# Token routing and dispatch in two sets, with the start of layer 2 for one set laid beside the last expert units, and expert weights loaded by DMA

## The chip, the core and the metric

The kernel runs on one core of a Trainium2 chip. A core has TensorE (PE, matmuls and transposes), VectorE (DVE), ScalarE (ACT, functions by table), GpSimd (POOL), and SyncE (SP), which issues most of the DMAs here. Each engine works through its own queue of instructions in program order, and engines wait for each other at semaphores. The metric is the time of one execution on the device, in microseconds (us); lower is better.

## The reference

The input is x, 16 sequences of 256 tokens of 128 floats (4096 tokens, all fp32). Two layers follow, both of the form x = x + s * silu(g) on normalised xn.

```python
xn = _layernorm(x)
# layer 0: attention per sequence; f is query, key and value
f = xn @ W.T + b
s = softmax(f @ f.T + distance_bias) @ f
# layer 0: a shared FFN and 8 routed experts, top 2 of sigmoid(logits)
shared = (silu(xn @ shared_gate.T) * (xn @ shared_up.T)) @ shared_down.T
w = top-2 scores per token, normalised to sum 1
combined = sum over the token's two experts: w * ((silu(xn @ gate_w) * (xn @ up_w)) @ down_w)
x = x + s * silu(shared + combined)
# layer 1 (called layer 2 below): token statistics attention, 16 heads of 8
xn = _layernorm(x)
w = xn @ Wqkv.T
logits = sum over d of (w / norm of w over the sequence)**2 * temp
Pi = softmax over heads(logits);  dots = sum over tokens of Pi_norm * w*w
s = (-(w * Pi) / (1 + dots)) @ Wout.T + bout
# layer 1: one expert per sequence, chosen by its last token
sel = argmax(softmax(gelu(last @ Wp1 + bp1) @ Wp2 + bp2))
out = (gelu(xn @ W1[sel] + b1) @ W2[sel] + b2) @ Wo + bo
x = x + s * silu(xn + 0.3 * out)
```

## The kernel before

**Tiles.** 4096 tokens are 32 tiles t of 128 (a token per partition), grouped in 8 chunks c of four tiles, which are two sequences b each. X holds x, XA the normalised tokens, XB a copy of them. Rows of XA and XB have 130 columns: 128 values, where the expert's result is to go, and the token's weight for it. XT is the transposed XA, FT and F are the projection f both ways, S the attention's output, SH the shared FFN's. PS0 to PS7 are the eight banks of PSUM.

**Order.** The order is written out by hand, engine by engine. Helpers of the same name on different engines are the parts of one step: `up(j)` is on TensorE the two matmuls of half a chunk, on ScalarE the SiLU (into SG), on VectorE the product (into HH).

1. *Start.* Per chunk: statistics (DVE L646), a root on ScalarE, `normalize` (DVE L657), four transposes (`turn_in`, PE L288, copied out by ScalarE), router logits (`logits`, PE L296), projection and its transpose (`project`, `turn_f`, PE L304 and L312). `spread_in`, `EARLY = 3` and `MID = 6` set which of them go before what.
2. *Routing.* When all 32 tiles have logits, VectorE finds the two experts of each token (`top`, twice, on 128x256 elements: 8 experts by 32 tiles), TensorE counts ranks with two matmuls (L329, L331), and VectorE turns them into places POS in a scratch buffer in DRAM (to L743), each expert's tokens padded to units of 128. EUI lists each unit's expert as an address (L749).
3. *Dispatch.* GpSimd scatters XA and XB, a tile at a time, in 64 indirect DMAs (L1230) into xs_scratch.
4. *Attention of layer 0*, 16 steps: scores on TensorE (L345), maximum on VectorE (L758 to L763), exponential on ScalarE (L1044), transposes (L357), `mix` (L370).
5. *Shared FFN*, the first `LATE = 5` chunks (PE L396 onwards).
6. *Experts.* SyncE fetches four units at a time (`fetch`) when all 64 scatters have landed. 71 units: transpose (`turn_x`, L441), eight gate and up matmuls per unit (L458; the "128x128 x568" in the profile), SiLU (ACT L1091), product (DVE L812), down matmuls (L472), output scaled (ACT L1098), scattered by GpSimd into yc_scratch (L1236). VectorE's `choose(u)` copies the unit's gate and up weights from WE, which holds all experts, into one of four buffers WC:

```python
r = e.value_load(EUI[0:1, u:u + 1], min_val=0, max_val=7 * 768)
e.tensor_copy(WC[:, u % 4, :], WE[:, bass.ds(r, 512)]).then_inc(s_wc, 1)
```

7. *Behind the experts.* The last three chunks of the shared FFN; 16 collects of yc; `end0(c)` adds the pairs of results and the shared part (DVE L823, L827) and takes the SiLU; GpSimd multiplies by S and, for odd chunks, adds into X (L1245).
8. *Head of layer 2*, all eight chunks in a pipeline: `stats1`, `norm1`, `turn1` (ACT L1131), `proj`, `squares` (two squares with a sum, ACT L1140, and a copy), `weigh`, `heads`, `center`, then the choice of 16 experts (`a1`, `a2`, SELI) and the softmax over heads (`soft`, `share`).
9. *Loop of layer 2*, b = 0 to 18, a sequence per step: `spread` every second step (PE transposes, ACT copy L1174, VectorE's sums L887 to L906), `out1` (PE L585), `ff_up` (L597), `ff_down` (L609), `ff_out`, `end_gate`, and the stores. SyncE loads each sequence's expert weights (`expert1`, 258 KB, L252).

## Time and profile before

| what | value |
|---|---|
| median of 3 runs | 371.18 us (369.55 to 375.51) |
| the profiled execution | 370.86 us, its span 369.0 us |
| TensorE busy | 301.6 us (82%) |
| VectorE busy | 222.2 us (60%) |
| ScalarE busy | 183.0 us (50%) |
| GpSimd busy | 184.1 us (50%) |
| granted TensorE clock, mean | 0.932 |

The span is the stretch from the first to the last instruction of the profiled execution, and its own time is 1.9 us above it. Busy shares are means over stages with different limits, so they say little alone: the rows below are by stage. The granted clock is the share of full speed (2.4 GHz) that TensorE was given; 0.5 is its lower level of 1.2 GHz.

### The profile page before, as it was taken

What the parts mean: (1) busy time and instruction counts of PE and PEld (TensorE: products, weight loads), DVE (VectorE), ACT (ScalarE), POOL (GpSimd) and SP (SyncE); (2) the same over time, 40 slices, a digit from 0 to 9 for tenths busy, and PEclk for the clock granted to TensorE, in tenths of its full rate; (3) what the DMA queues carried; (4) which work ended last, traced back from release to release, by engine and by line L of the source; (5) the groups of instructions that cost most, each with busy time, mean ns of one, the idle gap of its engine ahead of it and who ended that gap; (6) DMA issues with size and microseconds to landing.
All of it is one profiled execution on the core that took longest, in us unless ns stands there. A gap on an engine that the chain in (4) does not pass through costs nothing.

```text
span 369.0 us, 6792 instructions
## 1 busy us (share of the span) xinstructions
PE 301.6 (82%) x1933; PEld 250.9 (68%) x1933; DVE 222.2 (60%) x722; ACT 183.0 (50%) x482; POOL 184.1 (50%) x186
## 2 busy tenths in 40 slices
PE   0896599998998089999999999997448859987880
PEld 0684386776565079999999999865125647876770
DVE  5946846655222035555655555447999775778765
ACT  2356545555532025665565565523428765565450
POOL 1220277777777506666666577716965200142432
PEclk9999969999999759999999999998959967999996
DMA  6999931111111231332323232157000032234411
GB/s 195 248 208 146 370 143 54 54 56 51 51 52 51 68 91 35 108 106 70 105 73 105 67 103 65 37 186 272 1 0 0 1 95 55 81 110 103 136 57 57
DMA packets 33187, 35.66 MB, mean 97 GB/s; under 512 B 3824, under 2 KB 26482, under 8 KB 33024
## 3 DMA queue, kind: packets, MB, share of 16 engines
q1 hardware_dynamic: 28832, 26.76, 28.1%
q0 software_dynamic: 4320, 8.47, 6.9%
q8 instruction: 17, 0.28, 0.3%
q14 instruction: 18, 0.15, 0.1%
HBM read 19.87 MB, written 15.80 MB: 97 GB/s over the span
## 4 chain that ended last, share of the span: by engine, by line
PE 44%; DVE 22%; POOL 15%; issue 9%; ACT 4%; DMA 3%; SPq 1%; POOLq 0%; DVEq 0%
PE PS L458 18%; POOL xs_scratch L1230 15%; PE PS L472 9%; DVE XA L657 3%; PE PS L585 3%; DVE ST L646 2%; PE PS L441 2%; PE PS L609 2%; PE PS L296 2%; DVE XG L887 2%; DVE WE L906 2%; DVE SH L827 1%; PE PS L304 1%; PE PS L288 1%; DVE F L823 1%
## 5 line engine op out<-in xcount | busy, mean ns | idle before, releaser
L1236 POOL DMA_INDIRECT yc_scratch<-YS,XS x71 | 69.8, 983 | 45.5 <-ACT YS L1098 24.7
L458 PE MATMUL PS<-XG,XB 128*128 128x128 f32 x568 | 77.3, 281 | 0.7 <-ACT XG L1086 0.7
L458 PEld LDWEIGHTS PS<-XG,XB 128*128 128x128 f32 x568 | 71.4, 198 | 1.1 <-ACT XG L1086 1.1
L800 DVE COPY XB<-WE 128x512 f32 x71 | 30.9, 435 | 34.0 <-issue 33.1
L1091 ACT ACTIVATE FT<-PS 128x256 f32<-128x256 f32 x71 | 27.3, 384 | 39.8 <-PE PS L458 39.8
L812 DVE TENSOR_TENSOR FT<-FT,PS 128x256 f32<-128x256 f32 x71 | 29.9, 421 | 24.5 <-PE PS L472 16.4
L1230 POOL DMA_INDIRECT xs_scratch<-XA,POS x32 | 31.5, 983 | 26.4 <-DVE POS L743 17.0
L472 PE MATMUL PS<-WE,FT 128*128 x284 | 43.2, 275 | 0.2 <-DVE FT L812 0.2
L472 PEld LDWEIGHTS PS<-WE,FT 128*128 128x128 f32 x284 | 37.4, 192 | 0.4 <-issue 0.4
L1230 POOL DMA_INDIRECT xs_scratch<-XB,POS x32 | 31.3, 978 | 9.8 <-issue 9.8
L1258 POOL TENSOR_TENSOR F<-F,S 128x512 f32<-128x512 f32 x7 | 8.9, 1274 | 52.6 <-DVE F L937 52.6
L787 DVE TENSOR_TENSOR FT<-FT,PS 128x512 f32<-128x512 f32 x16 | 11.0, 687 | 29.2 <-PE PS L408 22.5
L1098 ACT ACTIVATE YS<-PS,XS 128x128 f32<-128x128 f32 x71 | 26.0, 366 | 3.9 <-PE PS L472 0.5
L1044 ACT ACTIVATE PR<-E,NM 128x256 f32<-128x256 f32 x32 | 16.0, 500 | 22.0 <-DVE NM L763 22.0
L370 PE MATMUL PS<-F,PT 128*128 128x128 f32 x128 | 18.9, 294 | 1.9
L441 PE MATMUL PS<-C,XS 128*128 128x128 f32 x71 | 11.6, 289 | 10.2 <-DMA XS<-xs_scratch 10.2
L370 PEld LDWEIGHTS PS<-F,PT 128*128 128x128 f32 x128 | 16.3, 200 | 5.0 <-DVE PT L772 5.0
L657 DVE TENSOR_SCALAR XA<-X,MV,RS 128x128 f32<-128x128 f32 x64 | 18.8, 357 | 0.6
L597 PE MATMUL PS<-XT,XS 128*128 128x256 f32 x64 | 18.2, 414 | 0.7 <-DMA XS<-in_w 0.7
L1245 POOL TENSOR_TENSOR F<-F,S 128x512 f32<-128x512 f32 x8 | 11.9, 1499 | 11.5 <-ACT F L1112 11.5
L345 PE MATMUL PS<-FT 128*128 128x256 f32 x64 | 17.6, 402 | 0.0
L609 PE MATMUL PS<-E,XS 128*128 128x256 f32 x64 | 17.0, 389 | 0.2 <-ACT PT L1192 0.2
(166 smaller groups left out, 600.4 us busy)
## 6 DMA issues: line engine op xcount, KB each, us to landing
xs_scratch<-ZB SPq DMA_DIRECT2D x1, 4680.0 KB, 28.6
XS<-xs_scratch SPq DMA_DIRECT2D x17, 260.0 KB
XS<-in_w SPq DMA_DIRECT2D x16, 258.0 KB, 2.9
WE<-in_we SPq DMA_DIRECT2D x1, 3072.0 KB, 16.7
X<-in_x SPq DMA_DIRECT2D x16, 128.0 KB, 2.4
XB<-yc_scratch SPq DMA_DIRECT2D x8, 256.0 KB, 4.4
WE<-yc_scratch SPq DMA_DIRECT2D x8, 256.0 KB, 6.0
out<-X SPq DMA_DIRECT2D x16, 128.0 KB, 2.1
```

Of the source, the lines that this page charges most:

```text
L370: m = e.matmul(PS[k][:, i * 128:(i + 1) * 128], PT[:, kb, j, i * 128:(i + 1) * 128], F[:, 2 * b + j, :], start=j == 0, stop=j == 1)
L441: m = e.transpose(PS[6][:, j * 128:(j + 1) * 128], XS[:, g % 4, j, 0:128], ident)
L458: m = e.matmul(PS[k][:, f * 128:(f + 1) * 128], WC[:, u % 4, f * 128:(f + 1) * 128], XG[:, g % 2, j * 128:(j + 1) * 128], start=True, stop ...
L472: m = e.matmul(PS[k][:, 0:128], HH[:, u % 3, f * 128:(f + 1) * 128], WE[:, bass.ds(reg[u] + (512 + f * 128), 128)], start=f == 0, stop=f == 1)
L609: m = e.matmul(PS[4][:, 0:256], WS[:, s, 256 + f * 128:256 + (f + 1) * 128], H1[:, b % 2, f, :], start=f == 0, stop=f == 1)
L657: m = e.tensor_scalar(XA[:, t, 0:128], X[:, t, :], MV[:, t, 0:1], RS[:, t:t + 1], ALU.subtract, ALU.mult)
L800: e.tensor_copy(WC[:, u % 4, :], WE[:, bass.ds(r, 512)]).then_inc(s_wc, 1)
L812: e.tensor_tensor(HH[:, u % 3, 0:256], SG[:, u % 3, 0:256], PS[u % 3][:, 256:512], ALU.mult).then_inc(s_hhe, 1)
L1091: e.activation(SG[:, u % 3, 0:256], PS[u % 3][:, 0:256], ACT.Silu, bias=0.0, scale=1.0).then_inc(s_sge, 1)
L1098: e.activation(YS[:, u % 8, :], PS[(5, 7)[u % 2]][:, 0:128], ACT.Copy, bias=0.0, scale=XS[:, g % 4, j, 129:130]).then_inc(s_ys, 1)
L1230: e.indirect_dma_start(out=xs, out_offset=bass.IndirectOffsetOnAxis(ap=POS[:, s, t:t + 1], axis=0), in_=T[:, t, :], in_offset=None, bounds ...
L1236: e.indirect_dma_start(out=yc, out_offset=bass.IndirectOffsetOnAxis(ap=XS[:, g % 4, j, 128:129].bitcast(U32), axis=0), in_=YS[:, u % 8, :] ...
```

## The change

**Two sets.** `CA = 4`: set 0 is the tokens of chunks 0 to 3, set 1 those of chunks 4 to 7. `choose(g)` (the top 2), `ranks(g)`, `positions(g)`, `experts(g)` and GpSimd's `dispatch(g)` exist for each set. Units of set 0 that are full come first (up to 32, `place(u)` gives a unit's place in the scratch), then eight units, one per expert, where set 0's remainders and set 1's first tokens share a unit, then set 1's. `FULL = 25`, `SHARED = 63`, `LAST_A = 40` (units whose results finish set 0) and `Y0 = 49` follow.

**Start and shared FFN.** TensorE, VectorE and ScalarE have a new order from the first chunk on. All eight chunks of the shared FFN come ahead of the attention, their `up` steps between the parts of the start. `project` and `turn_f` of chunks 4 to 7 stand in the attention's first steps. ScalarE makes the copies XB of chunks 4 to 7 (`copy_b`).

**Expert weights.** WE and VectorE's copies go. Down weights of all experts stay in WY; the gate and up weights of a unit are loaded by SyncE from DRAM (`weights(u)`, 256 KB) into the four buffers WC, at an address it reads from EI, once the unit four back is through. SyncE begins them after the last product and the last down of the shared FFN (`s_hh` 16, `p_dn` 8).

**Beside the last experts.** After unit 48's weights SyncE collects chunks 0 to 3. From unit 49 on VectorE does one part of `early(k)` behind each `hidden(u)` (the unit's product): per chunk `add_y`, `add_shared`, `gate_s`, `stats1`, and `norm1` of the chunk two back. ScalarE has the SiLU and two roots there.

**Behind the experts.** `norm1` of chunks 2 and 3 and layer 2's head for chunks 0 to 3 alone, then the loop. Adds, statistics, norms and head of chunks 4 to 7 stand behind the loop's steps b = 0 to 7, on VectorE, ScalarE and TensorE. GpSimd's products with S go to VectorE (`gate_s`). Eight head steps are done in one instruction per set. The buffers E, PR, PT lie in one tensor EP; ScalarE has 19 table loads in place of 8.

The first place is VectorE at the end of the routing: the places POS are ready, then the list of units' experts (in XG for a moment), and then comes the next step of the attention (L758).

```order
L739 TENSOR_REDUCE RW<-XS 128x32
L741 TENSOR_REDUCE RW<-XS 128x32
L743 CAST POS<-RW 128x64
L744 TENSOR_TENSOR XG<-C,RW 128x504
L747 TENSOR_REDUCE EU<-XG 128x72
L749 TENSOR_SCALAR EUI<-EU 128x72
L758 ISA E,RW<-PS,C 128x256
L758 ISA RW 128x1
```

In the changed kernel the same place is that of set 0. L753 is a product of the shared FFN, L734 and L737 are the norm of chunk 4.

```order
L878 TENSOR_REDUCE RW<-XS 128x16
L880 CAST POS<-RW 128x2x16
L753 TENSOR_TENSOR YS<-WC,PS 128x512
L888 TENSOR_TENSOR XG<-C,RB 128x504
L891 TENSOR_REDUCE EU<-XG 128x72
L899 TENSOR_SCALAR EI<-EU 128x72
L734 RECIPROCAL RS<-RS 128x4
L737 TENSOR_SCALAR XA<-X,MV,RS 128x128 x4
```

The shared FFN's product and the norms of chunks 4 to 7 now stand around and behind set 0's places, where the attention stood.

The second place is TensorE around the two rank matmuls (L329 and L331 before, L379 and L380 after). Before, projections (L304) and their transposes (L312) stand around them:

```order
L304 MATMUL PS4<-XT,WA 128x512
L312 MATMUL PS5<-C,FT 128x128 x4
L329 MATMUL PS7<-BFC 128x256
L331 MATMUL PS7<-BFC 128x256
L304 MATMUL PS3<-XT,WA 128x512
L312 MATMUL PS6<-C,FT 128x128 x4
```

After, L412 and L414 are the gate and up matmuls of the shared FFN, L355 the transposes of chunk 4's XA, L369 its logits:

```order
L390 MATMUL PS1<-XT,WA 128x512
L400 MATMUL PS7<-C,FT 128x128 x8
L379 MATMUL PS2<-BFC 128x128
L380 MATMUL PS2<-BFC 128x128
L412 MATMUL PS3<-XT,WB 128x512
L414 MATMUL PS4<-XT,WB 128x512
L355 MATMUL PS0<-C,XA 128x128 x4
L369 MATMUL PS7<-WA,XT 128x8 x4
L412 MATMUL PS5<-XT,WB 128x512
L414 MATMUL PS6<-XT,WB 128x512
```

Chunk 4's transposes, which were ahead of the ranks, now stand behind them and behind one `up` step, and each later chunk's logits follow its own transposes directly.

The third place is VectorE in the loop of layer 2. Before, the row L887 of a `spread` follows the FFN's part (L937, L914, L931) and the shares of a later chunk (L870 to L876) at once:

```order
L899 RECIPROCAL SM<-SM 128x2
L906 SCALAR_TENSOR_TENSOR WE<-PR,SM,FT 128x256 x2
L870 TENSOR_REDUCE WE<-WE 128x4
L872 RECIPROCAL WE<-WE 128x4
L876 TENSOR_TENSOR YS<-WE 128x512
L937 SCALAR_TENSOR_TENSOR F<-F,SH 128x512
L914 SCALAR_TENSOR_TENSOR S<-PS,WD 128x512
L931 SCALAR_TENSOR_TENSOR SH<-PS,SH 128x512
L887 ISA XG,SM<-PR,WE 128x256
```

After, at the end of step b = 2 and in b = 3 (L1111 and L1128 are the old L914 and L931):

```order
L975 TENSOR_TENSOR SH<-SH,F 128x512
L1111 SCALAR_TENSOR_TENSOR S<-PS1,WD 128x512
L1128 SCALAR_TENSOR_TENSOR SH<-PS7,SH 128x512
L981 TENSOR_TENSOR F<-F,S 128x512
L983 TENSOR_TENSOR X<-X,F 128x512
L726 BN_STATS ST<-X 128x6 x4
L729 BN_AGGR MV<-ST 128x2 x4
```

The adds of chunk 7 (L975) stand ahead of step 3's own work, and behind it `gate_s` and `stats1` of chunk 4; the last four rows come once more, for chunk 5, before the next `spread`.

The diff, cut to its core:

```diff
+CA = 4
+NTS = (4 * CA, NT - 4 * CA)
+FULL = 8 * CA - 7
+SHARED = NU - NE
+def place(u):
+    if u < 8 * CA:
+        return u
+    return u - 8 * CA + SHARED if u < 8 * CA + NE else u - NE
...
@@ SyncE
+            def weights(u):
+                if u >= 4:
+                    e.wait_ge(p_ge, u - 3)
...
+                    v = e.value_load(EI[0:1, g, place(u):place(u) + 1], min_val=0, max_val=7 * 256)
+                    of = D["wg"][bass.ds(v, 256)]
+                e.dma_start(WC[:, u % 4, :], of.rearrange("(p j) k -> p (j k)", j=2)).then_inc(d_wc[u % 4], 16)
...
-            e.wait_ge(d_disp, 16 * 2 * NT)
-            for g in range(NG):
-                fetch(g)
+            e.wait_ge(d_disp[0], 16 * 2 * NTS[0])
+            e.wait_ge(s_places, 2)
+            fetch(0)
+            e.wait_ge(s_experts, 1)
+            e.wait_ge(s_hh, 16)
+            e.wait_ge(p_dn, 8)
+            for u in range(4):
+                weights(u)
+            for g in range(1, 4):
+                fetch(g)
+            for u in range(4, NU):
+                weights(u)
+                g = u // 4 + 1
+                if u % 4 == 0 and 4 <= g < NG:
+                    fetch(g)
+                if u == LAST_A + 8:
+                    for i in range(8):
+                        e.wait_ge(d_y[i], 16 * (CA + 1))
+                    for c in chunks[0]:
+                        collect(c)
...
@@ TensorE
+            logits(3)
+            up(0)
+            up(1)
+            project(3)
+            turn_f(2)
+            turn_f(3)
+            ranks(0)
+            up(2)
+            turn_in(4)
+            logits(4)
+            up(3)
+            down(0)
+            turn_in(5)
+            logits(5)
+            up(4)
...
+            up(6)
+            up(7)
+            down(2)
+            ranks(1)
+            for j in range(8, 16):
+                up(j)
+                if j % 2 == 0:
+                    down(j // 2 - 1)
+            down(7)
...
             for i in range(NB + 2):
                 if i < NB:
                     scores(i)
+                if i < 4:
+                    project(4 + i)
                 if 1 <= i < NB + 1:
                     turn_p(i - 1)
+                if 1 <= i < 5:
+                    turn_f(3 + i)
                 if i >= 2:
                     mix(i - 2)
...
@@ VectorE
+            choose(0)
+            up(0)
+            positions(0)
+            up(1)
+            experts(0)
+            for c in range(CA, NC):
+                norm0(c)
+                up(c - CA + 2)
+            choose(1)
+            up(6)
+            up(7)
+            positions(1)
+            experts(1)
+            for j in range(8, 16):
+                up(j)
...
+            for u in range(NU):
+                hidden(u)
+                if u >= Y0:
+                    early(u - Y0)
+            for k in range(NU - Y0, 6 * CA):
+                early(k)
+            norm1(2)
+            norm1(3)
...
+                if b == 0:
+                    add_y(4)
+                    add_shared(4)
...
+                elif b == 3:
+                    for c in (4, 5):
+                        gate_s(c)
+                        stats1(c)
...
+                elif b == 5:
+                    norm1(4)
+                    norm1(5)
...
+                elif b == 7:
+                    weigh(1)
+                    select_max(1)
+                    center(1)
+                    select(1)
+                    sums(1)
+                    share(4)
+                    share(5)
...
@@ ScalarE
+                if b == 2:
+                    for c in chunks[1]:
+                        silu_l0(c)
+                elif b == 4:
+                    for c in chunks[1]:
+                        root1(c)
+                elif b == 5:
+                    turn1(4)
+                    turn1(5)
+                    squares(4)
...
@@ GpSimd
+            dispatch(0)
+            dispatch(1)
```

## Rows read from the trace of the kernel before

**Rows 1.** Busy us by stage; then granted clock, DMA share, GB/s.

```profile
93.00:130.00 37.00, 26.07 (x121) 16.20 (x120) 7.73 (x12) 10.52 (x18) 25.16 (x26) 0.92 0.20 63
130.00:237.80 107.80, 106.91 (x924) 106.32 (x925) 60.27 (x143) 61.82 (x159) 67.09 (x69) 0.96 0.29 80
237.80:302.40 64.60, 45.66 (x205) 28.95 (x205) 49.40 (x177) 32.05 (x89) 30.40 (x23) 0.86 0.21 71
302.40:330.60 28.20, 25.77 (x137) 22.36 (x138) 19.92 (x66) 15.71 (x44) 4.52 (x4) 0.89 0.32 92
330.60:369.00 38.40, 24.68 (x148) 21.11 (x146) 26.41 (x71) 16.83 (x44) 13.34 (x11) 0.92 0.31 90
```

**Rows 2.** Timeline, routing's end: start us, duration us, operation, [idle before].

```profile
36.62 0.42 DVE L705 TENSOR_TENSOR BFC<-XS 128x256 bf16<-128x256 f32 x1
42.65 0.20 DVE L743 CAST POS<-RW 128x64 int32<-128x64 f32 x1
43.80 1.16 POOL L1230 DMA_INDIRECT xs_scratch<-XA,POS  x1 [16.95 <-DVE POS L743]
44.30 0.41 DVE L758 CUSTOM_DVE_ANT_0 E<-PS,C 128x256 f32<-128x256 f32 x1
```

**Rows 3.** Two short stretches after it, columns as in rows 1.

```profile
42.90:46.40 3.50, 0.00 (x0) 0.00 (x0) 2.27 (x8) 1.28 (x5) 2.13 (x2) 0.89 0.96 414
46.40:52.60 6.20, 6.15 (x23) 5.48 (x24) 3.41 (x15) 2.81 (x10) 4.83 (x5) 0.51 0.45 174
```

**Rows 4.** Timeline of the shared FFN: TensorE's first matmul of two successive chunks.

```profile
104.60 1.02 PE L396 MATMUL PS<-XT,WB 128*128 128x512 f32 x2
109.82 1.02 PE L396 MATMUL PS<-XT,WB 128*128 128x512 f32 x2
```

**Rows 5.** Timeline of the attention: ScalarE's first exponential, TensorE's last mix.

```profile
45.31 0.51 ACT L1044 ACTIVATE PR<-E,NM 128x256 f32<-128x256 f32 x1 [2.22 <-DVE NM L763]
90.56 2.05 PE L370 MATMUL PS<-F,PT 128*128 128x128 f32 x16
```

**Rows 6.** Chain that ended last, where the experts start: start, duration, what.

```profile
124.81 2.30 DMA xs_scratch<-XB,POS
131.72 5.49 PE PS L458 x24
```

**Rows 7.** Groups by line: the experts' first matmul: busy us, mean ns | idle.

```profile
L458 PE MATMUL PS<-XG,XB 128*128 128x128 f32 x568 | 77.3, 281 | 0.7 <-ACT XG L1086 0.7
```

**Rows 8.** Page part 6 (us to landing), and SyncE's timeline issuing such loads.

```profile
XS<-in_w SPq DMA_DIRECT2D x16, 258.0 KB, 2.9
299.51 0.36 SPq L252 DMA_DIRECT2D XS<-in_w  x1
300.65 0.35 SPq L252 DMA_DIRECT2D XS<-in_w  x1
```

**Rows 9.** Timeline of ScalarE where it changes from exponential to SiLU.

```profile
93.29 1.28 ACT L1069 ACT_TABLE_LOAD   x1
94.59 1.24 ACT L1069 ACTIVATE FT<-PS 128x512 f32<-128x512 f32 x2
```

**Rows 10.** Groups by line, of layer 2's beginning: busy us, mean ns | idle.

```profile
L646 DVE BATCH_NORM_STATS2 ST<-X 128x6 f32<-128x128 f32 x64 | 13.8, 278 | 4.3 <-DMA X<-in_x 4.1
L657 DVE TENSOR_SCALAR XA<-X,MV,RS 128x128 f32<-128x128 f32 x64 | 18.8, 357 | 0.6
L823 DVE TENSOR_TENSOR F<-XB 128x512 f32<-128x512 f32 x4 | 2.8, 702 | 0.0
L1131 ACT ACTIVATE XT<-PS 128x512 f32<-128x512 f32 x8 | 4.8, 599 | 7.1 <-PE PS L524 7.1
L1140 ACT ACTIVATE WE<-PS 128x256 f32<-128x256 f32 x16 | 6.0, 384 | 1.9 <-PE PS L537 1.9
```

**Rows 11.** Timeline of VectorE in layer 2's loop: step b=0 and step b=8.

```profile
302.45 0.43 DVE L887 CUSTOM_DVE_ANT_0 XG<-PR,WE 128x256 f32<-128x256 f32 x1 [1.01 <-ACT PR L1174]
330.59 0.86 DVE L887 CUSTOM_DVE_ANT_0 XG<-PR,WE 128x256 f32<-128x256 f32 x1 [0.62 <-ACT PR L1174]
```

1215 lines of the change are left out of this document (673 added, 542 removed).

## The prediction

> **What bounds the kernel now.** Read the busy time by stage first [rows 1]. Between 130 and 237.8 us the experts run and TensorE is busy for 106.9 of 107.8 us: nothing else bounds there. Ahead of them TensorE is idle for 10.9 of the 37 us from 93 to 130. The chain of waits says why: it follows GpSimd's scatters up to the landing of the last one (124.81 + 2.30), then a fetch, and the first expert matmul starts at 131.72 [rows 6]. GpSimd starts at 43.80, once VectorE has the places at 42.65 [rows 2]. After the experts, from 237.8 to 302.4, VectorE is the busiest (49.4 of 64.6): the last three chunks of the shared FFN, then the norms and squares of all eight chunks. In layer 2's loop (302.4 on) VectorE is busy for 19.9 of 28.2 us, TensorE for 25.8, partly at the lower clock.
>
> So the change can win in two places: the 10.9 us ahead of the experts, and the 64.6 us behind them. It must not lengthen what leads to the experts, nor the loop.
>
> **A. Up to the first expert matmul.** Routing set 0 needs half-size steps. VectorE's steps on 256 elements take 0.42 us, those on 8 or 64 some 0.2 (one of each kind in [rows 2]), so one on 128 takes about 0.29; but finding the places of a set has seven steps more. I get 0.7 us more than half the old time for each set: 5.3 us for the places. With SiLU's table load in front of the first gate product, set 0's places are ready near 39.5 and GpSimd starts near 40.5, 3 us earlier; its 64 scatters take the same 83 us and end near 123.
>
> That does not set the experts' start, since TensorE's queue holds the whole shared FFN and all 16 attention steps ahead of the first turn_x. Against the old end of TensorE's queue (119.8 us: 93 + 26.07 busy in [rows 1]):
> - three chunks of the shared FFN come in front: 3 x 5.22 [rows 4] = +15.7;
> - old waits go: 3.3 for the mask (TensorE stands ahead of its rank matmuls; the mask's steps are those around 36.62 in [rows 2]), 3.5 for the first exponentials, and 3.1 since the 6.2 us behind that wait ran at half clock [rows 3]: -9.9;
> - new waits. up(2) waits for up(0)'s product, which on VectorE stands behind choose(0) and on ScalarE behind a table load: 2.8. turn_in(4) waits for norm0(4), which now stands behind positions(0), up(1) and experts(0): 5.3 + 0.7 + 1.6 (42.65 to 44.30, the steps behind the places [rows 2]) + 1.3 - 1.7 for up(2) = 7.1. An idle stretch of 3.5 us had cost the clock [rows 3], so this one should: +3.1. The logits of chunks 4 to 7 follow their own transposes with nothing between, 4 x 0.9 = 3.6. Set 1's places sit between up(7) and up(8): 1.5 + 4.1, and perhaps the clock again, +3. The last down waits for its product, 1.3. Sum +26.5.
> Attention takes 45.31 to 92.6 [rows 5], plus 2.8 for its start; the four project/turn_f pairs laid into its first steps hide in TensorE's gaps (2.15 us of work per 2.83 us step) apart from 2: +2. End of the queue: 119.8 + 15.7 - 9.9 + 26.5 + 2 = 154; fetch and weights lie ready; with the transpose and its copy the first expert matmul is at about 155. So A is **+22 to +23** (bounds 14 and 30: without the two clock losses and half of the waits, or with a third loss). GpSimd is idle by then: splitting the dispatch gives nothing here.
>
> **B. The experts.** Before: 131.72 to 237.8 with a half-clock start; without it 103 us, as a group of eight gate/up matmuls and its share of the rest take 1.45 us per unit [rows 7]. VectorE's copy of weights goes; it was not late, so it gives nothing. Instead SyncE loads 256 KB for each unit. It issues one such load in 1.14 us (299.51 to 300.65) and they land after 2.9 us [rows 8]. A load is issued when the unit four back is through, 4.9 us ahead of its use; 0.9 for the register and the issue, 2.9, and up to 1.3 when it queues behind a 260 KB fetch make 5.1. So I expect a few tenths lost at some units, 0 to 9 us in all, taken as 3. At unit 48 eight collects of yc take SyncE 3.7 us: one stall of 3. ScalarE's two table loads at unit 61: 1. B is **+4**: -3 for the clock, +7 (0 to 16).
>
> The DMA engines are busy for 0.32 of 28.2 us while nine such loads and a few stores run, so for at most 1.0 us per load, taken as 0.9; with the 0.29 of the experts' stage [rows 1] that makes 92% in 1.45 us per unit. The Trainium skill (DMA: Bandwidth & Descriptors, "Anatomy of one DMA") fits 2.0 us plus bytes at 436 GB/s for one transfer, 2.6 us for these loads, which is near the 2.9 here. By its 0.6 us for the bytes alone the engines would stand at 72% and the rival on the DMA would fall; the sum above does not use it.
>
> **C. From the experts' end to the loop**, before 64.6 us. Now the shared FFN is through, chunks 0 to 3 are added and mostly normalised beside the last 22 units (VectorE: 5.3 us in 8.7 us, beside 2.5 of products: it fits). Left: table load and roots 2.5; on ScalarE per chunk a copy 0.6, two squares with their sums 1.17, a copy 0.6 [rows 10] = 2.4, four chunks 9.6; the GELU table 1.6; then selection, heads, centring and shares in series, 7.6. 21.3 us in all (18 to 26). C is **-43**.
>
> **D. The loop's first half.** Step 0 to step 8 of VectorE took 302.45 to 330.59, 28.1 us [rows 11]. Now chunks 4 to 7 go through it: adds 8 x 0.70, gates and X adds 8 x 0.72, statistics 4 x 1.25, norms 4 x 1.3 [rows 10], selection and shares 5: 26 us on VectorE; 22 on ScalarE, 7.7 of it six table loads. If only VectorE's sum counted the half would take 19.9 + 26 - 1 = 45. But ScalarE's queue stops at silu_l0(7) for VectorE's adds and at root1(7) for the last statistics; step 5 stands until the transposes, projection and squares are back (4.6 us), step 7 for squares(7) (6.6), then for heads and a2 (2.5) and the exponentials (2): 15.7 idle. With 1.6 for GpSimd's adds beside VectorE's: 62. D is **+34** (+17 to +38). The second half keeps its 38.4 us.
>
> A change of function costs ScalarE a load of 1.28 us, and the next ACTIVATE starts 0.02 us behind it [rows 9], so the 11 loads that the change adds (19 for 8) cost 14 us of ScalarE. The Trainium skill (ScalarE: Activation LUTs, "What ACT_TABLE_LOAD costs") gives 2.66 us for a switch, 1.38 of it a drain. The load agrees with the trace, and behind it no drain shows. With one ahead of each load, the six in D and the two in C would make the time some 8 us longer (rival 4).
>
> **Sum.** 369.0 + 22.5 + 4 - 43 + 34 = 386 to 387 us of span. The profiled execution took 370.86 beside its span of 369.0, and the median is 371.18, so I add little: **387**.
>
> **The rivals.**
> 1. *The queues overlap* (faster). The mechanism: in-order engines meet ready operands, so in D only VectorE's sum counts (+17) and in A the new waits shrink to the one for norm0(4) (-14 with the clock losses). Decisive is whether step 8 comes within 45 us of step 0. For it: VectorE's idle 8.3 of 28.2 us in the loop. Against it: steps 5 and 7 have a round trip over three engines that nothing fills. 387 - 17 - 14 = 356.
> 2. *Half of that*: D at its low end alone, or A's waits at half and D somewhat shorter: 387 - 17 = 370, no change. For it: my waits are added one by one, and real queues absorb some.
> 3. *DMA takes over the experts.* 0.29 of 1.52 us, and 0.9 per load, make 1.34 of 1.45 us, and the collects 7 us more; queues at over 90% make late loads. It would add 10 to 15: 400.
> 4. *A drain ahead of every table load*, 8 us in C and D: 395. Against it: ScalarE is idle ahead of most of these loads anyway.
> 5. *The change does what it says*: experts start as set 0 is dispatched, near 84. It can't, the order of TensorE's queue forbids it; 1 in 100.
>
> **How the numbers follow.** Forecast 0.48, rival 1 0.09, rival 2 0.25, rival 3 0.14, rival 4 0.03, rival 5 0.01. A measurement here tells 2%, 7.4 us, from no change: below 363.8 faster, above 378.6 slower. Rival 1 is faster, rival 2 the same, the others slower. The range runs from 366, A and D near their low bounds, to 402, A and B at their high ones.
>
> **What would show it.** Right: TensorE idle for about 7 us near 36 to 43; first expert matmul at 148 to 162 while the last dispatch ended near 123; DMA share 0.7 to 0.9 in the experts; 19 to 24 us from the last expert matmul to VectorE's step 0; over 55 us to step 8. Wrong: an expert start before 145; a loop half under 50 us; experts over 120 us long (then rival 3).

## The result, and the profile after

The changed kernel takes 404.92 us (median of 4 runs, 403.89 to 407.87), the kernel before beside it 371.44 us (369.55 to 375.51). The ratio is 1.093 [1.085, 1.102]: slower by 9%, where 387 us (+4%) was forecast and 402 was the upper end of the range. The profiled execution took 403.89 us, its span is 402.0 us, the mean granted clock 0.906. Some executions of a kernel are over 1.5% slower than its fastest, and the traces of e5_bo, e7_collects and e9_res_serial below are of such ones, while ratios use the fast runs alone.

The stages are cut at the same events in both kernels: the first and the last gate and up matmul of the experts, VectorE's step b = 0 and step b = 8 of the loop, its last instruction, the end of the span. Us, from the timelines of both:

| stage | before | after | difference | forecast |
|---|---|---|---|---|
| A, to the first expert matmul | 131.7 | 152.3 | +20.6 | +22.5 |
| B, the experts | 104.2 | 116.9 | +12.7 | +4 |
| C, to step b = 0 | 66.5 | 28.0 | -38.5 | -43 |
| D, b = 0 to b = 8 | 28.1 | 62.2 | +34.1 | +34 |
| b = 8 to VectorE's last | 34.3 | 35.4 | +1.1 | 0 |
| to the end of the span | 4.1 | 7.1 | +3.0 | 0 |

The differences add up to the 33.0 us between the spans. (C was forecast from the down matmuls' end, 237.8, which moves 1.8 us from C to B in both kernels.)

The last four rows together are 132.7 us after and 133.0 before. Behind the last gate and up matmul of the experts the change gives nothing: what C gives, D and the end take back. The whole loss of 33 us lies in A and B.

Windows of the changed kernel, columns as in [rows 1]: all of A, the stretch of the start that the forecast spoke of, the experts, two stretches in them, C, D, and the rest.

```profile
0.00:152.30 152.30, 119.84 (x600) 83.73 (x600) 78.06 (x325) 66.65 (x166) 66.70 (x77) 0.93 0.30 93
36.00:44.00 8.00, 3.53 (x7) 1.35 (x6) 7.53 (x30) 0.60 (x1) 2.72 (x3) 0.50 0.05 17
152.30:269.20 116.90, 105.48 (x909) 103.85 (x910) 41.93 (x113) 65.94 (x164) 65.33 (x67) 0.97 0.78 237
170.00:219.00 49.00, 46.58 (x406) 45.52 (x406) 13.04 (x31) 27.16 (x70) 30.18 (x31) 1.00 0.86 255
219.00:234.00 15.00, 7.69 (x69) 7.50 (x68) 2.52 (x6) 4.99 (x13) 6.82 (x7) 0.89 0.93 315
269.20:297.30 28.10, 17.34 (x80) 12.69 (x79) 14.69 (x43) 15.07 (x43) 9.09 (x9) 0.73 0.38 115
297.30:359.50 62.20, 38.10 (x190) 29.23 (x189) 42.79 (x140) 33.35 (x84) 10.45 (x8) 0.83 0.09 23
359.50:402.00 42.50, 27.68 (x152) 23.83 (x152) 24.52 (x67) 18.05 (x45) 12.76 (x10) 0.86 0.32 93
```

The same window of A in the kernel before:

```profile
0.00:131.70 131.70, 99.60 (x526) 72.81 (x526) 66.67 (x267) 57.15 (x149) 68.72 (x81) 0.95 0.51 128
```

So in A TensorE has 20.2 us more of busy time, and is idle for 32 us in both kernels. TensorE is idle for 11.4 of the 116.9 us of the experts, where it was idle for 0.9 of 107.8 [rows 1]. In the 15 us from 219 it works half the time while the DMA engines stand at 0.93. In D VectorE is the busiest and is still idle for 19.4 us.

The start, from the timeline; it answers to [rows 2, 3, 6]:

```profile
35.11 2.04 PE L412 MATMUL PS<-XT,WB 128*128 128x512 f32 x2 [3.33 <-DVE WC L753]
39.54 0.18 DVE L880 CAST POS<-RW 128x32 int32<-128x32 f32 x1
40.67 1.26 POOL L1503 DMA_INDIRECT xs_scratch<-XA,POS  x1 [24.16 <-DVE POS L880]
43.33 1.11 PE L355 MATMUL PS<-C,XA 128*128 128x128 f32 x4 [4.47 <-DVE XA L737]
121.80 0.97 POOL L1503 DMA_INDIRECT xs_scratch<-XB,POS  x1 [0.30 <-issue]
152.32 2.94 PE L549 MATMUL PS<-XG,WC 128*128 128x128 f32 x24 [0.69 <-ACT XG L1325]
```

The last scatter is issued at 121.80 and the experts start 30 us later. What lies between is TensorE's own queue.

The experts: the group that answers to [rows 7], then SyncE and TensorE around unit 48, from the timeline.

```profile
L549 PE MATMUL PS<-XG,WC 128*128 128x128 f32 x568 | 77.2, 280 | 12.1 <-DMA WC<-in_wg 9.6 <-ACT XG L1325 2.0 <-issue 0.3
```

```profile
216.60 4.81 SPq L276 DMA_DIRECT2D WC<-in_wg  x4
221.51 0.38 SPq L261 DMA_DIRECT2D XS<-xs_scratch  x1
222.19 4.06 SPq L282 DMA_DIRECT2D XB<-yc_scratch  x8
227.34 3.67 SPq L276 DMA_DIRECT2D WC<-in_wg  x4
...
233.87 2.08 PE L549 MATMUL PS<-XG,WC 128*128 128x128 f32 x8 [7.31 <-DMA WC<-in_wg]
```

Of the 9.6 us on the weights' DMA one wait takes 7.31: the weights of the next unit were issued at 227.34, behind the eight collects, and landed 6.5 us later. The matmuls behind the wait ran at half clock, 2.08 us for 1.06. The remaining 2.3 us are four short waits.

Behind the experts (C), the same timeline; the norms answer to L657 in [rows 10].

```profile
272.71 1.11 DVE L737 TENSOR_SCALAR XA<-X,MV,RS 128x128 f32<-128x128 f32 x4
273.94 3.92 DVE L737 TENSOR_SCALAR XA<-X,MV,RS 128x128 f32<-128x128 f32 x4
274.93 2.32 POOL L1519 TENSOR_TENSOR SH<-XA,BO 128x512 f32<-128x512 f32 x2
277.98 2.00 DVE L737 TENSOR_SCALAR XA<-X,MV,RS 128x128 f32<-128x128 f32 x4
...
286.14 0.17 DVE L1024 TENSOR_SCALAR SM<-SM 128x8 f32<-128x8 f32 x1 [1.35 <-ACT F L1381]
287.00 5.36 PE L609 MATMUL PS<-HB,F 128*128 128x16 f32 x32 [2.58 <-DVE HB L1030]
292.39 0.42 DVE L1037 TENSOR_REDUCE MX<-PS 128x16 f32<-128x256 f32 x1 [3.20 <-PE PS L609]
297.27 0.43 DVE L1084 CUSTOM_DVE_ANT_0 XG<-EP,F 128x256 f32<-128x256 f32 x1 [1.48 <-ACT EP L1423]
```

The norm of a chunk, four instructions, takes 1.11 us alone, 3.92 beside two of GpSimd's additions of bout and 2.00 beside one. The head's 32 small matmuls take 5.36 us at a lower clock.

D, VectorE in the loop and, as the third row, the head matmuls of the second set; the last row is step b = 8 and answers to [rows 11].

```profile
334.89 0.43 DVE L1084 CUSTOM_DVE_ANT_0 XG<-EP,F 128x256 f32<-128x256 f32 x1 [5.00 <-ACT EP L1423]
346.34 0.69 DVE L1111 SCALAR_TENSOR_TENSOR S<-PS,WD 128x512 f32<-128x512 f32 x1 [4.74 <-PE PS L651]
350.19 3.81 PE L609 MATMUL PS<-HB,F 128*128 128x16 f32 x32
354.17 0.15 DVE L1054 TENSOR_TENSOR SEL<-PS,WD 8x8 f32<-8x8 f32 x1 [4.06 <-PE PS L624]
359.47 0.43 DVE L1084 CUSTOM_DVE_ANT_0 XG<-EP,F 128x256 f32<-128x256 f32 x1 [1.48 <-ACT EP L1423]
```

VectorE's three long waits are the round trips over ScalarE and TensorE in steps 5 to 7. The same 32 head matmuls take 3.81 us here and 5.36 in C.

### The profile page after: what moved, and what is told of

Read it like the earlier page. It is cut to its first block, busy times and chain, and to the rows that moved or that the text cites. A ratio compares the mean times of both kernels' runs of the same rounds, so it can differ in the third digit from the quotient of the medians.

```text
span 402.0 us, 6909 instructions
## 1 busy us (share of the span) xinstructions
PE 308.4 (77%) x1927; PEld 253.3 (63%) x1927; DVE 202.0 (50%) x686; ACT 199.1 (50%) x498; POOL 164.3 (41%) x170
## 4 chain that ended last, share of the span: by engine, by line
PE 44%; DVE 25%; ACT 10%; DMA 8%; issue 7%; SPq 3%; DVEq 0%; ACTq 0%; POOLq 0%
PE PS L549 12%; DMA WC<-in_wg 6%; PE PS L564 5%; DVE XA L737 3%; PE PS L425 3%; PE PS L412 3%; PE PS L414 3%; ACT EP L1298 2%; PE PS L609 2%; PE PS L369 2%; DVE EP L936 2%; PE PS L390 2%; PE PS L677 2%; PE PS L601 2%; DVE OT L1103 2%
## 5 line engine op out<-in xcount | busy, mean ns | idle before, releaser
L549 PE MATMUL PS<-XG,WC 128*128 128x128 f32 x568 | 77.2, 280 | 12.1 <-DMA WC<-in_wg 9.6
L549 PEld LDWEIGHTS PS<-XG,WC 128*128 128x128 f32 x568 | 70.3, 195 | 14.0 <-DMA WC<-in_wg 11.1
L964 DVE TENSOR_TENSOR EP<-EP,PS 128x256 f32<-128x256 f32 x71 | 29.7, 419 | 78.5 <-PE PS L564 44.7
L1332 ACT ACTIVATE EP<-PS 128x256 f32<-128x256 f32 x71 | 27.2, 383 | 46.5 <-PE PS L549 46.5
L564 PE MATMUL PS<-WY,EP 128*128 (+1 forms) x284 | 43.7, 277 | 0.2 <-DVE EP L964 0.2
L564 PEld LDWEIGHTS PS<-WY,EP 128*128 128x128 f32 x284 | 37.7, 194 | 0.4 <-issue 0.4
L412 PE MATMUL PS<-XT,WB 128*128 128x512 f32 x32 | 19.2, 684 | 8.1 <-DVE WC L753 4.4
L737 DVE TENSOR_SCALAR XA<-X,MV,RS 128x128 f32<-128x128 f32 x64 | 23.5, 434 | 0.6
L1298 ACT ACTIVATE EP<-EP,NM 128x256 f32<-128x256 f32 x32 | 16.0, 500 | 14.7 <-DVE NM L941 14.7
L677 PE MATMUL PS<-EP,XS 128*128 128x256 f32 x64 | 18.4, 415 | 3.1 <-ACT EP L1441 3.1
L506 PE MATMUL PS<-F,EP 128*128 128x128 f32 x128 | 18.0, 285 | 1.6
L414 PE MATMUL PS<-XT,WB 128*128 128x512 f32 x32 | 18.7, 671 | 0.0
L355 PE MATMUL PS<-C,XA 128*128 128x128 f32 x32 | 7.3, 370 | 14.7 <-DVE XA L737 14.7
L506 PEld LDWEIGHTS PS<-F,EP 128*128 128x128 f32 x128 | 15.4, 191 | 4.4 <-DVE EP L950 4.4
```

The source lines that it names most:

```text
L412: e.matmul(PS[k][:, :], WB[:, f * 128:(f + 1) * 128], tile(XT, 4 * c, 4), start=True, stop=True).then_inc(p_g, 1)
L414: e.matmul(PS[k + 1][:, :], WB[:, 256 + f * 128:256 + (f + 1) * 128], tile(XT, 4 * c, 4), start=True, stop=True).then_inc(p_u, 1)
L506: m = e.matmul(PS[k][:, i * 128:(i + 1) * 128], PT[:, kb, j, i * 128:(i + 1) * 128], F[:, 2 * b + j, :], start=j == 0, stop=j == 1)
L549: m = e.matmul(PS[k][:, f * 128:(f + 1) * 128], WC[:, u % 4, f * 128:(f + 1) * 128], XG[:, g % 2, j * 128:(j + 1) * 128], start=True, stop ...
L564: m = e.matmul(PS[k][:, 0:128], HHE[:, u % 3, f * 128:(f + 1) * 128], w, start=f == 0, stop=f == 1)
L677: m = e.matmul(PS[6][:, 0:256], WS[:, s, 256 + f * 128:256 + (f + 1) * 128], H1[:, b % 2, f, :], start=f == 0, stop=f == 1)
```

## The experiments

In the runs from e8_res_norms to e20_after the kernel before itself took 448 to 454 us instead of 371; the last section shows where the time goes. There only kernels that were run side by side are compared, and of the stages only C and D. The kernel before has its usual times in these (68.0 and 27.8 us in e19_before), the changed kernel somewhat longer ones (30.9 and 65.9 in e20_after for 28.0 and 62.2), so a difference of a few us between two single traces is not read from them.

### The experts: late loads, the collects, or VectorE's copies

**e1_eight.** The changed kernel with eight weight buffers in place of four (the other four in XT, which is free then), loads issued eight units ahead.

```diff
-                if u >= 4:
-                    e.wait_ge(p_ge, u - 3)
+                if u >= 8:
+                    e.wait_ge(p_ge, u - 7)
...
-                e.dma_start(WC[:, u % 4, :], of...).then_inc(d_wc[u % 4], 16)
+                e.dma_start(slot(u), of...).then_inc(d_wc[u % 8], 16)
```

> Eight weight buffers in place of four, so a load may be issued eight units ahead of its use instead of four. The changed kernel took 404.9 us, its experts' stage 117 us (152.3 to 269.3), with 9.7 us of TensorE's waits on weight loads. Theory 1, lead and order in SyncE's queue: the loads are late because one is issued only four units ahead and stands behind fetches and eight collects; with eight units of lead (10.7 us) all these waits go and the stage takes 106 to 108 us; time 394 to 396. Theory 2, bandwidth: the DMA engines stand at 0.86 to 0.93 in this stage and can't go faster; waits stay for the most part, the stage takes 112 us or more; time 399 to 404.

Measured: 398.46 us (394.36 to 399.26), 1.075 [1.062, 1.087] of the kernel before. The group of the first matmul, half of it per tensor, and the window from 200 to 240:

```profile
L557 PE MATMUL PS<-XG,XT 128*128 128x128 f32 x280 | 38.1, 281 | 2.2 <-DMA XT<-in_wg 2.2
...
200.00:240.00 40.00, 37.83 (x324) 37.64 (x323) 14.50 (x38) 22.09 (x57) 24.62 (x25) 0.96 0.93 304
```

The stage takes 107.0 us for 116.9, as the first theory had it (106 to 108); the time lies between the two expectations. The waits on weights fall from 9.6 to 2.2 us with the same bytes, so distance and not the volume made most of them late. The DMA engines still stand at 0.93 in that window, and the one wait that is left, 2.2 us at 232.80, comes behind the eight collects, which SyncE issues from 221.18 on.

**e7_collects.** Only the collects are moved: a chunk's two after every second unit from 48 on, not eight at once.

```diff
-                    for c in chunks[0]:
-                        collect(c)
+                if u >= LAST_A + 8 and (u - LAST_A - 8) % 2 == 0 and (u - LAST_A - 8) // 2 < CA:
+                    collect((u - LAST_A - 8) // 2)
```

> The eight collects of chunks 0 to 3 are issued two at a time behind the weights of units 48, 50, 52 and 54 in place of all eight behind unit 48. Theory 1, order in SyncE's queue: the 7.3 us stall at unit 49 shrinks to 1 or 2 us, with the clock that it cost; time 398 to 400. Theory 2, bandwidth: the same 2 MB still have to pass beside the loads, the stall is cut into several of the same sum; time 403 to 405.

Measured: 397.85 us (395.25 to 404.49), 1.073 [1.063, 1.084] of the kernel before, 7 us less than the changed kernel.

```profile
L549 PE MATMUL PS<-XG,WC 128*128 128x128 f32 x568 | 76.2, 278 | 8.0 <-DMA WC<-in_wg 5.9 <-ACT XG L1325 2.0
```

The waits fall by 3.7 us and the experts' stage by 4.7 (112.2); the clock in the stage is 1.00 where it was 0.97. The eight collects ahead of the next weights in SyncE's queue were the largest single cost, as the first theory had it. The second has a part too: the wait of 7.31 us became four between 230 and 246 us, together 2.7, and 5.9 us of waits on weights are left in the stage.

**e2_resident.** The gate and up weights of all experts lie in WC, and VectorE copies a unit's into XT, as the kernel before did. Everything else is the change.

```diff
-            for u in range(4):
-                weights(u)
+            e.dma_start(wc_flat.rearrange("p (j e k) -> p j e k", j=2, e=NE),
+                        D["wg"].rearrange("(e p j) k -> p j e k", e=NE, j=2)).then_inc(d_wc[0], 16)
...
             for u in range(NU):
+                if u + 2 < NU:
+                    choose_w(u + 2)
                 hidden(u)
```

> Gate and up weights of all experts stay in SBUF, and VectorE copies each unit's weights as in the kernel before; no weight load per unit. DMA share in the stage falls to about 0.3 in both theories. Theory 1, VectorE has no room for copies beside the last 22 units: it would need 0.42 for the product, 0.44 for the copy and about 1.0 for a part of early per unit, 1.9 us against 1.34, so the first 49 units gain 9 us and the last 22 lose 8 to 12; time 402 to 408. Theory 2, the copies hide as before: the stage falls to 107 and the time to 394 to 396.

Measured: 392.59 us (391.82 to 394.09), 1.063 [1.053, 1.074]. The experts, and the group of the first matmul:

```profile
152.00:257.50 105.50, 103.02 (x912) 102.13 (x913) 69.22 (x181) 66.26 (x165) 67.20 (x68) 1.00 0.31 96
```

```profile
L535 PE MATMUL PS<-XG,XT 128*128 128x128 f32 x568 | 75.3, 276 | 3.2 <-ACT XG L1331 1.6 <-DVE XT L1011 1.4
```

My theory that VectorE has no room for the copies beside the `early` steps fell. It has 36 us to spare, and TensorE waits 1.4 us for it in all. So the weights by DMA cost 12 us and bought nothing; with eight buffers (e1_eight, 107.0) they would cost 2 us of the stage. The stage is 105.1 us long at full clock; before it was 104.2 with a half-clock start [rows 1, 6]. The 2.4 us in which TensorE is idle all lie in the last 40 us, beside `early`: 1.4 for the copies, 0.95 behind ScalarE's two table loads.

### Between the experts and the loop, and the loop

**e5_bo.** The changed kernel, with GpSimd's additions of bout held back until VectorE has the head's scales:

```diff
                 e.wait_ge(s_xn, c + 1)
+                e.wait_ge(s_hb, c // CA + 1)
                 e.tensor_tensor(four(XNB, c), four(XA, c), BO3[...]...)
```

> GpSimd's adds of the bias (plus_bo) wait until the head weights of their set are done, so that they don't run beside VectorE's last norms. In the changed kernel the norms of chunks 2 and 3 took 3.9 and 2.0 us where 1.1 is usual, both beside such adds. Theory 1, the two engines slow each other: the norms take 1.1 each, the stretch from the last expert matmul to the loop falls from 28.0 to 24.5 us, and the two norms in the loop lose 1.7 us more; time 400 to 401. Theory 2, the norms are slow for another reason: no change, 404 to 406.

Measured: 403.12 us (400.69 to 408.86), 1.089 [1.076, 1.101], not to be told from the changed kernel. The norms of chunks 1 to 3 from its timeline:

```profile
277.89 1.11 DVE L737 TENSOR_SCALAR XA<-X,MV,RS 128x128 f32<-128x128 f32 x4
279.13 1.12 DVE L737 TENSOR_SCALAR XA<-X,MV,RS 128x128 f32<-128x128 f32 x4
280.36 1.11 DVE L737 TENSOR_SCALAR XA<-X,MV,RS 128x128 f32<-128x128 f32 x4
```

All norms are back at 1.11 us, and C takes 26.1 us in place of 28.0: of the 3.7 us taken from VectorE, 1.9 reach the stage, while the head matmuls behind them take 7.01 us here for 5.36. GpSimd's additions were the cause of the long norms. The Trainium skill (SBUF — State Buffer, "Who interferes with whom") gives a reason for such a pair: VectorE's tensor_scalar can run in a mode that takes both port pairs, and then it and GpSimd contend for the shared pair, which the first to issue holds for its whole instruction. These rows agree with it in that a norm is long only beside a GpSimd addition (3.92 and 2.00 us for 1.11); that the ports are the reason, no run here shows.

**e9_res_serial.** e2_resident with the whole head of chunks 4 to 7 ahead of the loop, as before the change; only the experts' end keeps its `early` steps.

```diff
             sums(0)
+            for c in chunks[1]:
+                add_y(c)
+                add_shared(c)
+            for c in chunks[1]:
+                gate_s(c)
+                stats1(c)
+            for c in chunks[1]:
+                norm1(c)
+            weigh(1)
```

> Base as above (from loop step 0 at 284.5 to step 8 at 346.9 is 62.4 us). The whole head of layer 2 for chunks 4 to 7 stands ahead of the loop, in one piece; the loop then has nothing else in it. Theory 1, laying this work between the loop's steps hides some of it (VectorE is busy for 42.8 of 62.4 us there, and was for 19.9 of 28.1 in a loop of its own): undone, the work takes some 32 us alone and the loop's half 28, so C and D together stay within 3 us of 89.4; time 390 to 395. Theory 2, the in-order queues make the mixture slower than its parts in a row: C and D together fall to 80 to 84; time 383 to 387. Theory 3, the mixture hides much: 8 or more us slower, time over 400.

Measured: 479.49 us (475.99 to 484.28), 1.076 [1.057, 1.095]; e8_res_norms beside it is at 463.85 us and 1.045. C and D together take 74.5 + 32.3 = 106.7 us, and 27.5 + 64.0 = 91.5 in e8_res_norms, 89.8 in e2_resident. C:

```profile
335.70:410.10 74.40, 38.27 (x139) 26.18 (x138) 36.98 (x124) 32.69 (x83) 9.06 (x9) 0.58 0.14 44
```

So laying set 1's head into the loop does hide work, 15 us of it, and the two medians differ by as much (15.6): the third theory held. But the kernel before needs 66.5 + 28.1 = 94.6 us for both without any of this, since its eight chunks go through one pipeline beside the shared FFN. Cut in two sets and run in series, the head is worse than before (clock 0.58, TensorE idle for 36 us); layered, it ends 3 to 5 us ahead. That lead is lost again behind step b = 8, where e2_resident takes 36.5 + 7.0 us and the kernel before 34.3 + 4.1.

**e10_res_norm1.** e2_resident with the four norms of set 1 all in step b = 5.

```diff
                 elif b == 5:
-                    norm1(4)
-                    norm1(5)
-                elif b == 6:
-                    norm1(6)
-                    norm1(7)
+                    for c in chunks[1]:
+                        norm1(c)
```

> Base as above. All four norms of chunks 4 to 7 stand at step 5 of the loop, where VectorE waits 5.0 us for ScalarE behind two of them; their roots are there by then. Theory 1, the place of the work in the queue is what costs the loop: the half gets 4 to 6 us shorter (62.4 to 57 or 58); time 387 to 389. Theory 2, the wait only moves (ScalarE and TensorE set the pace there): under 2 us; time 391 to 393.

Measured: 464.27 us (456.32 to 470.43), beside 450.4 for the kernel before, too spread for an interval. D is 59.2 us, 62.4 in e2_resident and 64.0 in e8_res_norms beside it. It is 59.7 to 60.4 in the seven other runs that hold this edit and 62.2 to 66.0 in all that do not (e9_res_serial, whose loop is another, left out). So 2 to 4 us of D was the order of the norms, between what the two theories had; the rest stays.

### The start

**e8_res_norms** (e2_resident with this edit), **e4_norms** and **e16_norms** (the changed kernel with it): the norms of chunks 4 and 5 ahead of set 0's places.

```diff
             choose(0)
+            norm0(4)
+            norm0(5)
             up(0)
             positions(0)
             up(1)
             experts(0)
-            for c in range(CA, NC):
+            up(2)
+            up(3)
+            for c in range(CA + 2, NC):
```

> Base: the kernel with resident expert weights (392.6 us; first expert matmul at 152.0). VectorE norms chunks 4 and 5 ahead of the product of up(0) and of set 0's places, where it stands idle for 2.2 us on ScalarE. Theory 1, the order of VectorE's queue costs the start 4.5 us of waits for norm0(4) and a stretch of TensorE at half clock: the first expert matmul comes at 144 to 147; time 385 to 388. GpSimd's dispatch starts up to 1 us later, which changes nothing. Theory 2, another wait takes its place (up(3) for its product, the logits' banks): first expert matmul within 2 us of 152; time 390 to 393.

> The changed kernel itself (404.9 us, first expert matmul at 152.3, weights by DMA) with the norms of chunks 4 and 5 ahead of the product of up(0) and of set 0's places. The same edit on the kernel with resident weights brought chunk 5's logits 7 us forward (46.1 against 53.3) in a run whose start was then held up elsewhere. Theory 1: first expert matmul at 144 to 147, time 397 to 400. Theory 2, a later wait takes it back (set 1's places, the attention): first expert matmul at 150 to 152, time 402 to 405.

> The changed kernel with the norms of chunks 4 and 5 ahead of set 0's places, again for the same reason. In its first 50 us the logits of chunk 5 came at 39.9 in place of 53.3. Theory 1, the gain reaches the experts: first expert matmul at 140 to 145, time 394 to 399. Theory 2, a later wait takes it back: 149 to 152, time 401 to 405.

(The 39.9 us there is the time of chunk 4's logits, which are at 45.12 in the changed kernel.) Measured, in ratios to the kernel before beside each: e8_res_norms 463.85 us, 1.045 [1.030, 1.060]; e4_norms 471.49 us, 1.035 [1.025, 1.045]; e16_norms 480.34 us, 1.058 [1.051, 1.065]. The window from 36 to 44 in e4_norms:

```profile
36.00:44.00 8.00, 7.31 (x32) 4.36 (x32) 6.30 (x24) 2.31 (x4) 2.48 (x3) 0.79 0.03 10
```

TensorE works for 7.3 of these 8 us, for 3.5 in the changed kernel, and chunk 4's logits come 5 us earlier: the wait for norm0(4) is what held it. Whether the experts start earlier for it these runs cannot say. In them TensorE stands during the scatters, and the first expert matmul came at 204.0 in e8_res_norms, beside 201.6 in e10_res_norm1, without the edit, and 202.8 in e12_all, with it. e4_norms and e16_norms are the same kernel 2% apart in ratio, so nothing under that is read from this condition.

### All of it together, and a start of another order

**e12_all, e14_all, e17_all** are one kernel: e2_resident with the edits of e8, e10 and e5, and `a2(1)` ahead of `heads(1)`.

> Base as above, with the norms of chunks 4 and 5 ahead of set 0's places, all norms of step 6 at step 5, the bias adds on GpSimd behind the head weights, and a2(1) ahead of heads(1) on TensorE, so that the second eight experts are chosen 3.7 us sooner (step 8's ff_up waits for their weights). If the costs are independent: -6 for the start, -5 for the norms, -2 to -3 for the bias adds, -2 for the choice; time 376 to 379. If they hide behind one another: 381 to 385. The kernel before takes 371; if this reaches it, splitting can be made to break even by order alone.

> The same kernel as the one with resident weights and all four reorderings, whose first runs fell on a chip where also the kernel before took 450 us. Without that hold-up: first expert matmul at 144 to 147, experts 105, 26 to the loop, 59 to 60 for its first half, 42.5 for the rest: 376 to 379 if the four costs are independent, 381 to 385 if they hide behind one another.

> Resident weights and all four reorderings on the changed kernel, again for the same reason. First expert matmul at 140 to 145, experts 105, 28 to the loop, 60 for its first half, 43.5 for the rest: 376 to 382 if the start's gain is kept, 385 or more if not.

Measured: 459.05, 461.25 and 469.94 us, ratios 1.035 [1.021, 1.048], 1.019 [1.012, 1.026] and 1.037 [1.029, 1.046]. They lie below that of the changed kernel, but whether the four costs add up or hide behind one another cannot be read from them.

**e13_hybrid, e15_hybrid, e18_hybrid, e21_hybrid** are one kernel: e12_all with a new start. The shared FFN stands behind the attention, set 1's routing is cut in small pieces that stand between the attention's steps, and the projections come ahead of it.

```diff
@@ TensorE
+            for j in range(16):
+                up(j)
+                if j % 2 == 0 and j > 0:
+                    down(j // 2 - 1)
+            down(7)
@@ VectorE
+                if i < 5:
+                    run(ch, 4)
+                elif i == 5:
+                    run(ch)
+                    ch = positions(1)
+                    ex1 = experts(1)
+                elif i < 11:
+                    run(ch, 5)
```

> Resident weights, the later part as in the run with all four reorderings, and a new start: on TensorE the transposes and logits of set 0 first, then the rest of the start, the attention, and the whole shared FFN behind it, as in the kernel before; on VectorE the norms of chunks 4 to 7 in its idle time, set 0's places ahead of the attention, and set 1's routing cut into four or five instructions per attention step. Theory 1, the order of the start and not the two sets makes the first expert matmul late: it comes at 133 to 138 (before: 131.7, with three chunks of the shared FFN less ahead of it), then 105 for the experts, 26 to the loop, 59 for its first half, 42.5 for the rest: time 366 to 371 where the kernel before takes 371. Theory 2, routing in two sets costs by itself, wherever it stands: VectorE's 12 us beside the attention lengthen it by as much, first expert matmul at 145 or later, time 377 or more.

> The kernel with the new start, again, since on the chip of its first run also the kernel before took 454 us and every engine but GpSimd stood for tens of us during the dispatch, so that its start could not be read. Its first 45 us could: GpSimd's dispatch started at 36.8 and the attention at 44.3. Theory 1, the order of the start makes the first expert matmul late, and not the two sets: 133 to 138, time 364 to 371. Theory 2, set 1's routing beside the attention lengthens it by its own 12 us: 145 or later, time 377 or more.

> The new start once more, to read it undisturbed if the chip allows it. Theory 1: first expert matmul at 133 to 138, time 364 to 371, below the kernel before. Theory 2: 145 or later, time 377 or more.

> The new start for the last time. If the kernel before beside it takes about 371 us again: first expert matmul at 133 to 138 and a time of 364 to 371 by theory 1 (the order of the start makes the experts late), 145 or later and 377 or more by theory 2 (the routing in two sets does). If it takes about 450 again, only the ratio is read, which has been 1.015 to 1.026, and the question stays open.

Measured: 461.32, 465.9 and 459.85 us, ratios 1.017 [1.010, 1.023], 1.026 [1.017, 1.035] and 1.015 [1.008, 1.022]; then, with the kernel before at 370.64 us, e21_hybrid 383.06 us (381.98 to 386.04), 1.039 [1.027, 1.052]. Its stages are 145.9, 105.2, 27.5, 60.3, 36.3 and 6.8 us. The last 48 us ahead of its experts:

```profile
98.00:146.00 48.00, 45.54 (x217) 29.09 (x218) 14.04 (x25) 18.60 (x36) 20.22 (x21) 1.00 0.09 31
```

Behind the attention TensorE is the limit: at full clock it is busy for 45.5 of 48 us, while GpSimd's last scatter was issued at 123.3. In the attention it is not. ScalarE's first and last exponential and TensorE's matmul that waits for them, in e21_hybrid:

```profile
43.40 0.51 ACT L1346 ACTIVATE EP<-EP,NM 128x256 f32<-128x256 f32 x1
98.16 0.49 ACT L1346 ACTIVATE EP<-EP,NM 128x256 f32<-128x256 f32 x1
L462 PE MATMUL PS<-C,EP 128*128 128x128 f32 x64 | 10.5, 287 | 15.3 <-ACT EP L1346 15.3
```

and in the kernel before, whose first exponential is at 45.31 [rows 5]:

```profile
89.12 0.49 ACT L1044 ACTIVATE PR<-E,NM 128x256 f32<-128x256 f32 x1
L357 PE MATMUL PS<-C,PR 128*128 128x128 f32 x64 | 11.3, 303 | 5.1 <-ACT PR L1044 5.0
```

The attention takes 54.8 us between these exponentials where it took 43.8, and VectorE's steps of set 1's routing stand between its own. The second theory of these four runs expected this: the routing beside the attention lengthens it by its own 12 us, first expert matmul at 145 or later, 377 us or more. Both numbers are met, and those of the first (133 to 138, 364 to 371) are missed. The old end of TensorE's queue, the three chunks and the longer attention give 119.8 + 15.7 + 11.0 = 146.5 for the 145.9 measured. The three chunks alone would end the queue near 135.5, only 4 us behind the old start of the experts, because they fill the wait for the last scatter. So of the 14.2 us that A still has over the kernel before some 11 go with the routing of set 1. That is read from the trace; no run leaves this routing out. e21_hybrid is the best version with two sets, 22 us faster than the changed kernel, and no version found beats the kernel before.

**e19_before** and **e20_after** are the two given kernels in the other condition.

> The kernel before itself, for its profile in the condition in which it takes 450 us. If the hold-up is one of the dispatch, as in the traces of the changed kernels, the first expert matmul comes near 205 in place of 131.7 and the stretches behind the experts are within 2 us of those of the first trace; then rows behind the experts can be compared between the two conditions, and those ahead of them only within one.

> The changed kernel itself in the same condition, as the base for the runs on the start. Theory 1, the start costs it as much here as there: first expert matmul 15 to 20 us behind that of the kernel before, ratio 1.06 to 1.08. Theory 2, the hold-up of the dispatch hides the cost of the start: first expert matmul at about the same time as before's, ratio 1.04 or less.

Measured: 448.06 us (one run), and 474.4 us (468.49 to 482.18) beside 450.95 for the kernel before, 1.05. There e20_after's first expert matmul comes at 200.5 and e19_before's at 191.7: A differs by 8.8 us and not by 20.6, between the two theories. Probably TensorE's queue is no longer all that this stage waits for; no run tests it.

## Why the prediction was wrong in size

**What bounds the kernel** was read rightly. The experts start when TensorE's queue reaches them, 29.5 us after the last scatter, and its 20.2 us more of busy time ahead of them are nearly the whole of A.

**A held** (+20.6 for +22.5). Places at 39.54 (39.5), GpSimd from 40.67 (40.5), the last scatter over at 122.8 (123), first expert matmul at 152.3 (155). The waits that were set at 2.8 for up(2) and 7.1 for turn_in(4) are 3.33 and 4.47, with the clock at 0.50 around them. Those around set 1's places, 1.5 and 4.1, are 1.07 and 3.66. (The 119.8 for the old end of the queue is right by the trace; the sum written beside it, 93 + 26.07, gives 119.1.) No run takes A apart: e21_hybrid has the three chunks as well, but another order and a longer attention.

**B was wrong, +12.7 for +4.** The step that failed is "at unit 48 eight collects of yc take SyncE 3.7 us: one stall of 3". SyncE took 4.06 for them, but the stall was 7.31: the step counted the queue time and not that the next weights then need 6.5 us to land, behind eight collects in DMA engines that are at 0.93. That these collects are the cause is shown by e7_collects. The term of 3 for small delays held (2.3), and the table loads at unit 61, set at 1, cost 1.32. The clock behind the stall had no term: the matmuls of the next units take some 2 us more. About 2 us of B are not accounted for. Rival 3 had the place and the sign; its 10 to 15 us over the forecast were 8.7. Its reason, a queue without room, is right for the stretch of the collects alone, since e1_eight removes most of the waits with the same bytes. The DMA share that the prediction put at 92% from its rows was 0.86 from 170 to 219 us.

**"It was not late, so it gives nothing"**, of VectorE's copy, held in the stricter sense: e2_resident has it beside the `early` steps for 1.4 us of waits.

**C was too good by 4.5.** Of that 1.9 are the norms beside GpSimd's additions, shown by e5_bo; the sum for C had no term for them. The rest is in "selection, heads, centring and shares in series, 7.6": it took 11.1 (286.14 to 297.27). Of these 3.5 us the clock explains some 1.6: the 32 head matmuls take 5.36 us, behind 17.8 us in which TensorE was idle for 7.9, and 3.81 at 350.19, where the clock is 0.97. That is read from the rows, not tried by itself. The other 2 us stay open.

**D held** (62.2 for 62), and its mechanism with it: single waits of 5.0, 4.7 and 4.1 us in steps 5 to 7 (4.6, 6.6 and 4.5). That the sum is right to 0.2 us is luck, for VectorE was busy for 42.8 us (45, and 1.6 beside GpSimd) and idle for 19.4 (15.7). e10_res_norm1 shows 2 to 4 us of it to be order. Rival 1, in which the queues overlap and only VectorE's sum counts, was wrong; e9_res_serial shows that the overlap is real, 15 us, and already part of the 62.

**"The second half keeps its 38.4" failed, 42.5.** 1.1 us come ahead of VectorE's last instruction: step b = 8 waits for expert weights that SyncE issues only at 356.81 and runs below full clock. The other 3 lie behind it, 7.1 for 4.1, in e2_resident and e21_hybrid as well (7.0 and 6.8). The same instructions end both kernels, and in both the DMA engines have nothing more to do some 1.3 us behind VectorE's last instruction. Which wait lengthens the end after it stays open; it was not tried.

**Rival 4 fell.** In C a table load of 1.28 us at 271.45 stands 0.02 us behind ScalarE's last instruction and is followed by its root at 272.74, 0.01 us behind it. The other loads show no gap of that kind either. The 19 loads add no drain of 1.38 us each, which is the Trainium skill's figure (ScalarE: Activation LUTs, "What ACT_TABLE_LOAD costs").

The sum of the misses: B +8.7, C +4.5, the end +4.1, A -1.9, D 0: 15.4 us, near the 18 by which the median is above 387 (the rest is the 1.9 us of the profiled execution outside its span, less the 0.5 by which the forecast was rounded up, and the 1.0 by which the median is above that execution).

## What to carry to other kernels

Splitting work in two sets pays only where the first set's start was what the bounding engine waited for. Ask first whether that engine's queue has room to be shorter; here it had not, and what had filled TensorE behind the experts moved in front of them. Add up all stages behind the one that gets shorter: C lost 38.5 us, and everything behind the experts together 0.3. Small steps laid between those of a stage that waits on the same engine can make it longer, as set 1's routing seems to have done with the attention in e21_hybrid. A wait behind a queue costs the queue's time, the landing of the next transfer and the clock lost after it: price all three, and do not put bulk transfers in one go ahead of loads that are due each microsecond and a half.
